# Tables rebuilt on chip for the second pass, diagonal matrices on VectorE, and the mixing inputs loaded by ScalarE's queue

## What is computed

```python
x = x + einsum('bct,bcd->bdt', x, weights[cond])       # mixing: one of 16 matrices per batch
K = 2 * einsum('hn,hnl->hl', Ct, exp(dtA * arange(2048))).real   # 64 complex modes per channel
y = irfft(rfft(x, 4096) * rfft(K, 4096))[..., :2048] + x * D     # causal convolution per channel
x = x + y * (arange(2048) < length[:, None])
```

## Time and profile before

| | us |
|---|---|
| median of 3 runs (lowest, highest) | 1109.16 (1108.6, 1116.84) |
| profiled execution | 1110.37 |
| its span | 1108.4 |
| PE busy in the span | 1021.2 (92%) |
| VectorE busy | 768.2 (69%) |
| ScalarE busy | 573.6 (52%) |
| GpSimd busy | 635.0 (57%) |
| HBM read, written | 171.25 MB, 147.00 MB |

### The profile page before, as it was taken

How to read it: one execution, slowest core, us unless ns; L and a number is a source line. 1 busy time by engine, 2 the same in 40 slices (tenths; PEclk the granted TensorE clock), 3 DMA queues, 4 the chain that set the end, 5 groups by cost and what they waited for, 6 DMA issues and landing times.

```text
span 1108.4 us, 33416 instructions
## 1 busy us (share of the span) xinstructions
PE 1021.2 (92%) x12910; PEld 793.0 (72%) x12910; DVE 768.2 (69%) x1754; ACT 573.6 (52%) x1275; POOL 635.0 (57%) x1377
## 2 busy tenths in 40 slices
PE   8877784889898999899999999999999999999998
PEld 5332242457676667698898988888889888988986
DVE  4989930447565556577777787777777777777775
ACT  2634352335454444456566565555565555555554
POOL 3201136955566465276765868658686676757740
PEclk9999997889999999999999999999999999999999
DMA  9999999899999999989999999999999999899994
GB/s 342 415 408 416 418 414 389 295 361 362 394 372 386 372 388 341 327 211 292 208 261 255 260 264 220 260 226 258 280 229 255 239 254 280 206 263 217 267 215 125
DMA packets 225277, 330.93 MB, mean 299 GB/s; under 512 B 60306, under 2 KB 105746, under 8 KB 216930
## 3 DMA queue, kind: packets, MB, share of 16 engines
q1 hardware_dynamic: 224802, 328.34, 96.9%
q0 software_dynamic: 160, 0.20, 0.1%
q10 hardware_dynamic: 160, 0.26, 0.1%
HBM read 171.25 MB, written 147.00 MB: 287 GB/s over the span
## 4 chain that ended last, share of the span: by engine, by line
PE 74%; DMA 19%; ACT 2%; issue 2%; SPq 2%; DVE 1%; DVEq 0%; ACTq 0%
PE bank L834 15%; PE bank L852 14%; PE bank L796 12%; DMA u_scratch<-stage 10%; PE bank L773 10%; PE bank L813 7%; PE bank L751 7%; DMA u_row<-u_scratch 6%; PE bank L840 5%; PE bank L739 3%; DMA gt_scratch<-gt_sb 2%; ACT stage L935 1%; DMA x_f<-in_x 1%; SPq L400 1%; DVE o_sb L1253 0%
## 5 line engine op out<-in xcount | busy, mean ns | idle before, releaser
L852 PE MATMUL bank<-g_sb,st_sb 128*128 128x256 f16 x1536 | 308.4, 274 | 0.3 <-issue 0.3
L773 PE MATMUL bank<-ident,u_row 128*128 128x128 f32 x1024 | 279.1, 276 | 19.4 <-DMA u_row<-u_scratch 18.3
L636 POOL TENSOR_TENSOR g_sb<-g_x,g_sb 128x128 f16<-128x128 f32 x256 | 115.9, 487 | 265.1 <-ACT g_sb L920 265.1
L964 ACT ACTIVATE st_sb<-bank 128x128 f16<-128x128 f32 x448 | 124.1, 277 | 252.5 <-PE bank L813 182.2
L1253 DVE COPY_PREDICATED o_sb<-mask,u_row 128x512 f32<-128x512 uint8 x256 | 199.1, 778 | 16.2 <-issue 16.0
L1236 DVE TENSOR_TENSOR st_sb<-bank,st_sb 128x128 f16<-128x128 f32 x448 | 130.2, 291 | 113.7 <-ACT st_sb L964 107.7
L1231 DVE SCALAR_TENSOR_TENSOR u_t<-bank,u_t 128x512 f16<-128x512 f32 x256 | 176.0, 688 | 44.4 <-ACT u_t L948 43.5
L834 PE MATMUL bank<-toep,u_t 128*128 128x192 f16 (+1 forms) x1752 | 198.0, 221 | 1.8 <-issue 1.8
L948 ACT ACTIVATE u_t<-bank 128x512 f16<-128x512 f32 x256 | 151.4, 592 | 48.2 <-PE bank L773 48.1
L773 PEld LDWEIGHTS bank<-ident,u_row 128*128 128x128 f32 x1024 | 144.7, 142 | 31.3 <-DMA u_row<-u_scratch 20.8
L739 PE MATMUL bank<-x_f,w_buf 128*128 128x512 f32 x280 | 130.7, 616 | 35.9 <-issue 24.5
(11 more groups left out here) (142 smaller groups left out, 1527.8 us busy)
## 6 DMA issues: line engine op xcount, KB each, us to landing
x_f<-in_x SPq DMA_DIRECT2D x64, 1024.0 KB, 13.4
u_scratch<-stage SPq DMA_DIRECT2D x128, 512.0 KB, 11.3
u_row<-u_scratch SPq DMA_DIRECT2D x128, 512.0 KB, 5.6
out<-o_sb SPq DMA_DIRECT2D x510, 128.0 KB, 3.7
toep<-k_scratch SPq DMA_DIRECT2D x16, 512.0 KB, 7.8
g_scratch<-g_sb SPq DMA_DIRECT2D x12, 512.0 KB, 7.3
gt_scratch<-gt_sb SPq DMA_DIRECT2D x12, 512.0 KB, 7.7
toep_later<-k_scratch SPq DMA_DIRECT2D x24, 256.0 KB, 6.3
```

Of the source, the lines that this page charges most:

```text
L773: ins = pe.transpose(bank[:, u_bank(s, v), k % 4 * P:(k % 4 + 1) * P], ap(u_row[b], v * UNIT + g * Q + tb * P, [[1, P]]), ident[:, :])
L852: last = pe.matmul(bank[:, y, col:col + Q], st_sb[s % 2][:, v, a, gr * P:(gr + 1) * P], g_sb[t % GS][:, h, b, :], start=False, stop=(m == ...
```

## The change

- The second copies of the 12 wide tables are no longer stored and loaded. `store_g`, `load_g`, `load_gt`, `stored_g` and the waits on them go. POOL makes every table when its slot comes, the 24 of the `part` 1 slots too, and `transpose_g` transposes them by DMA.
- A list `MADE_AT` says which tables POOL makes in slot c: those of slot c+2 up to slot 12, later those of slot c+3.
- All diagonal matrices are made by DVE at place 5.2; POOL makes none.
- In slots 0 to 9, ACT issues the loads of `x` right behind its evacuations (`load_x(act, ...)` in `unit_evac`), no longer SP. SP's `load_u(c+1, 1)` moves from behind the four stores at k=0 to before them at k=1.
- Up to slot 10, DVE's overlay of (c-1, 1) moves from place 5.1 to 4.2, and the output work of (c-1, 2) from 7.1 to 6.2 and 6.3.
- The stage buffers of batch 34 are 6 and 7, not 0 and 1.

```diff
+MADE_AT = [[] for _ in range(NSL + 2)]
+for s in range(2, NSL):
+    MADE_AT[s - 2 if s <= LATER + 2 else s - 3] += TABS[s]
...
-STAGE_AT = [m % STAGES if m < 2 * NBW else m % (STAGES // 2) for m in range(2 * NB)]
+STAGE_AT = [m % STAGES for m in range(2 * NBW)] + [0, 1, 2, 3, 6, 7] + [m % (STAGES // 2) for m in range(2 * NBW + 6, 2 * NB)]
...
             if last is not None:
                 eng.wait_ge(s_st, 7 * SLOT_OF[last] + 1)
-                stored_g(eng, last)
...
+        def load_x(eng, n):
+            last = before(X_AT, n)
+            if last is not None:
+                batch_mixed(eng, last)
+            eng.dma_start(x_f[X_AT[n]][:, :], x[n, :, :]).then_inc(s_x[X_AT[n]], 16)
...
             def mixing_slot(c):
                 for k in range(8):
-                    if k == 0:
-                        if c > 0:
-                            load_toeplitz(c)
+                    if k == 0 and c > 0:
+                        load_toeplitz(c)
+                    if k == 1:
+                        load_u(c + 1, 1)
                         if has(c - 2):
                             store_out(sp, c - 2, 1)
-                        load_u(c + 1, 1)
-                    if k == 1:
-                        store_g(c)
...
                     if k == 5:
+                        if c == 0:
+                            stages_landed(sp, (6, 7), NB)
                         load_u(c + 2, 0)
...
-                        if UNITS[u].batch and q == 3 and n + 3 < NB:
-                            load_x(n + 3)
...
-                if c < WIDE:
-                    store_g(c)
                 if c + 1 >= WIDE and has(c + 1):
-                    if SLOTS[c + 1].made:
-                        transpose_g(c + 1)
-                    else:
-                        load_gt(c + 1)
+                    transpose_g(c + 1)
...
                     load_toeplitz(c + 2)
-                    if not SLOTS[c + 2].made:
-                        load_g(c + 2)
...
             def slot(c):
-                if has(c + 2) and SLOTS[c + 2].made:
-                    for t in TABS[c + 2]:
-                        outer(t)
-                if has(c + 1) and not lam_by_dve(c + 1):
-                    for t in TABS[c + 1]:
-                        make_lambda(t)
+                for t in MADE_AT[c]:
+                    outer(t)
...
-                if has(c + 2) and SLOTS[c + 2].made:
-                    for t in TABS[c + 2]:
-                        outer_lo(t)
+                for t in MADE_AT[c]:
+                    outer_lo(t)
...
             def unit_evac(u):
 
                 to, half = unit_copy(act, u)
                 act.activation(to, half, ACT.Copy).then_inc(s_ev, 1)
+                for w in (u - 1, u):
+                    if w >= PROLOGUE and UNITS[w].batch and UNITS[w].part == 3 and UNITS[w].of + 3 < NB:
+                        load_x(act, UNITS[w].of + 3)
...
-                steps = [(0.0, "s", c - 1, 7), (0.1, "u", c, 3), (0.2, "o", c - 2, 3), (0.3, "g", c + 2, 0),
+                steps = [(0.0, "s", c - 1, 7), (0.1, "u", c, 3), (0.2, "o", c - 2, 3), (0.3, "g", c, 0),
...
-                         (4.0, "s", c, 3), (4.1, "u", c + 1, 1), (5.0, "s", c, 4), (5.1, "o", c - 1, 1),
-                         (5.2, "l", c + 1, 0), (6.0, "s", c, 5), (6.1, "u", c + 1, 2), (7.0, "s", c, 6), (7.1, "o", c - 1, 2)]
+                         (4.0, "s", c, 3), (4.1, "u", c + 1, 1), (5.0, "s", c, 4),
+                         (5.1 if c > LATER else 4.2, "o", c - 1, 1), (5.2, "l", c + 1, 0), (6.0, "s", c, 5),
+                         (6.1, "u", c + 1, 2), (7.0, "s", c, 6), (7.1 if c > LATER else 6.3, "o", c - 1, 2)]
...
-                        elif lam_by_dve(of):
+                        else:
                             make_lambda(of)
```

More of the change, by code:

```diff
@@ L2 @@
 from contextlib import ExitStack
-from itertools import accumulate
 from typing import NamedTuple
@@ L57 @@
     part: int
-    made: bool
-SLOTS = [Slot(True, 4 * i, 0, True) for i in range(WIDE)]
+SLOTS = [Slot(True, 4 * i, 0) for i in range(WIDE)]
 for i in range(H // 2 - 2 * WIDE):
-    SLOTS.append(Slot(False, H1 + 2 * i, 0, True))
+    SLOTS.append(Slot(False, H1 + 2 * i, 0))
     if i % 3 == 2 and i // 3 < WIDE:
-        SLOTS.append(Slot(True, 4 * (i // 3), 1, False))
+        SLOTS.append(Slot(True, 4 * (i // 3), 1))
 NSL = len(SLOTS)
@@ L75 @@
         SLOT_OF.append(s)
-MADE_NO = list(accumulate([0] + [int(SLOTS[s].made) for s in SLOT_OF]))
+MADE_AT = [[] for _ in range(NSL + 2)]
+for s in range(2, NSL):
+    MADE_AT[s - 2 if s <= LATER + 2 else s - 3] += TABS[s]
 GT_AT = [t % 2 if t < 2 * WIDE else t % 4 for t in range(len(PAIR_OF))]
@@ L369, in landed_with @@
             return t0 if t > t0 and TOEP_AT[t0] % 4 < 3 and TOEP_AT[t] == TOEP_AT[t0] + 1 else t
-        def loads_of_g(t):
-            return sum(not SLOTS[SLOT_OF[r]].made for r in range(t % GS, t + 1, GS))
         def unit_copy(eng, u):
@@ L406, in _ @@
             sp.dma_start(w_f[:, :, :], w_in.rearrange("s c d -> c s d")).then_inc(s_in[2], 16)
-            def load_x(n):
-                last = before(X_AT, n)
-                if last is not None:
-                    batch_mixed(sp, last)
-                sp.dma_start(x_f[X_AT[n]][:, :], x[n, :, :]).then_inc(s_x[X_AT[n]], 16)
             def store_half(n, j):
@@ L503, in _ @@
             for n in range(1, XS):
-                load_x(n)
+                load_x(sp, n)
             for n in range(FIRST):
@@ L787, in inputs_to_state @@
                         b = GT_AT[t]
-                        landed = sum(32 if SLOTS[SLOT_OF[r]].made else 16 for r in range(2 * WIDE, t + 1) if GT_AT[r] == b)
-                        pe.wait_ge(s_gt[b], landed)
+                        pe.wait_ge(s_gt[b], 32 * (GT_AT[2 * WIDE:t].count(b) + 1))
                 wait(pe, s_stl, 7 * s)
@@ L991, in slot @@
                         unit_evac(of)
+                    elif what == "g":
+                        for t in MADE_AT[of]:
+                            g_hi(t)
                     elif has(of):
@@ L998, in slot @@
                             out_evac(of, k)
-                        elif what == "t":
+                        else:
                             fold_toeplitz(of)
-                        elif SLOTS[of].made:
-                            for t in TABS[of]:
-                                g_hi(t)
             slots(slot)
```

100 lines of the change are left out of this document (25 added, 75 removed).

## The result

The changed kernel takes 1145.78 us in the median of four runs (1143.45 to 1150.53), the kernel before 1113.0 in four (1108.6 to 1120.32). The ratio is 1.029, with a 95% interval of 1.022 to 1.037: slower, as forecast, but by 32.8 us between the medians where the forecast had 15.1, and 0.8 us above the upper end of the range. The profiled execution took 1150.53 us with a span of 1148.4, 40 us more than the span before.

A forecast was written before the change was run, and what follows sets the result against it. PE was taken to bound the long last stretch; the mixing slots held 24 us of waits or low clock. From 1110.37 us, -19 + 21.6 + 12.5 = +15.1 gave 1125.5, median 1124; range 1097 to 1145.

The forecast's parts named there:

- (1): Slots 11 to 62: VectorE's matrices between the states of steps 4 and 5 make PE wait, +21.6 us.
- two matrices take 402.73 - 401.53 = 1.20, one 0.60: Duration of VectorE's diagonal matrix, read in the mixing slots and used past them: 0.60 us each.
- (2): Twelve slots 12 to 56: ScalarE waits 1.96 us for GpSimd's second table, PE about 1.04 us each; +12.5 us.
- the 1.41 us of rows 10: VectorE's idle time before a slot's first state, taken as room that absorbs part of ScalarE's 2.50 us lateness.
- Rival C: Past the mixing: GpSimd slows beside VectorE's new instruction, outer product 6.6 us; +13 us, 1137 us; chance 0.12.
- The mixing slots, -19: Slots with mixing: table-store waits go and waits for rows shrink, -19 us of 24 us idle or low clock.
- the end of -8: Low end of the mixing gain: only slot 10's wait goes, since the DMA engines stay full; -8 us.
- rival B: Mixing slots: the DMA engines stay the bound, -8 us instead of -19, whole 1135 us; chance 0.12.
- I take 1.5 us of these 1.9: Mixing slots: earlier overlay brings the load of rows forward by 1.5 us, leaving 0.4 us of wait per slot.
- their entry at nothing: Mixing slots: ScalarE's 28 issues of x at 0.65 us each counted as costing nothing; uncovered 18 us.
- 13.6: Predicted length of slot 10 without waits, in us.
- no PE wait on them shows: Past the mixing: DMA queues lose 48 loads and gain 48 transposes; 0, at most 2 us either way.

The follow-up runs named there:

- e9: Changed kernel with GpSimd's table instructions past slot 10 cut to two columns, later tables not computed; span 1106.4 us, groups of four slots 48.1 us.
- e2: Kernel before with VectorE making all diagonal matrices, tables still stored and loaded; span 1141.9 us, eleven groups 541.2 us against 517.4.
- e6: Changed kernel with x loads on SyncE, that of step 3 held until the rows are issued at step 5; span 1130.0 us, slots 1 to 11 219.1.
- e1: Changed kernel with the 25 mixing-slot loads of x back on SyncE at their old place; span 1141.9 us, slots 1 to 11 228.7.
- e8: Changed kernel with the mixing slots' whole old order, table stores still gone; span 1140.9 us, slots 1 to 11 224.8.
- e11: Second profile of the kernel of e8; span 1136.6 us, slots 1 to 11 222.8.
- e12: Second profile of the unmodified changed kernel; span 1148.5 us, slots 1 to 11 232.1.
- e3: Changed kernel with three g_x buffers, not two, GpSimd making up to two outer products ahead past slot 10; span 1128.0 us, eleven groups 543.8.

## Why the prediction was right or wrong, point by point

- **Direction: right. Mechanisms: right past the mixing, half right in it.** Both losses past the mixing are there, each at its place: the matrix between two states, and twelve waits of ScalarE on GpSimd of 1.86 us on average (1.96 predicted). In the mixing slots the wait on a table store went, but PE's waits for rows did not.
- **(1), the matrices, +21.6: too small.** The step that failed is "two matrices take 402.73 - 401.53 = 1.20, one 0.60". That row lies where GpSimd stood still (its last instruction there ended at 399.5), and beside a working GpSimd the instruction takes longer: 0.68 and 0.94 us in the 16 and 2 matrices of the mixing slots of the kernel before, so its own trace had the difference. Past the mixing the mean is 0.89 to 0.92 us. The other steps held: without GpSimd beside the matrix a narrow slot lost 0.21 us, in e9 and in e2 (0.31 predicted); with it 0.7. e2 gives the term as 23.8 us in the eleven groups, 27.7 with slots 11 to 15 and 59 to the end (+2.4, +1.5).
- **(2), the second table, +12.5: too small.** The wait itself was sized well, and what PE loses by it was not: 16.4 us in the eleven groups, 1.5 for each and not 1.04. With slot 12, where slots 11 to 15 took 1.7 us more than in e2, it is about 18. The overlay and the matrix on VectorE were longer too, so there may have been less room than the 1.41 us of rows 10; what the missing half microsecond is was not tried.
- **Rival C** named the right cause, GpSimd and VectorE in each other's way, and looked at the wrong engine. Its condition came true: from 520 to 1040 us an outer product took GpSimd 4 x (0.496 + 0.542 + 0.635) = 6.7 us, where C had 6.6, but by the same count it took 6.5 in the kernel before, and ScalarE's waits were no longer than forecast. The dear part was the slower VectorE, in the state chain. The Trainium skill (GPSIMD Engine Reference, Specifications) has the two share SBUF interfaces, with contention when VectorE reads two SBUF inputs; e9's 0.68 us against 0.92 agrees.
- **The mixing slots, -19: too large**, 9.2 measured in the profiled runs, near the end of -8 and so near rival B's time, though not by B's cause: e6 shows that the DMA engines had room for 219 us. The step that failed is "I take 1.5 us of these 1.9" for the earlier overlay, which was to leave 0.4 us of wait in a slot. The load was issued 2 us earlier and landed 0.3 us earlier, because a load of `x` stood right ahead of it (with `x` behind it, in e6, it landed 2.9 us earlier than before the change); PE's waits for rows between 200 and 470 us went from 18.3 to 17.7 us, and the 3.45 us of slot 0 became 4.2. ScalarE's issues of `x` took 0.34 us each, and there were 25, not 28: their entry at nothing is not refuted, since e1, with `x` back on SyncE, has the same landing times. The removed stores alone gave what was forecast for the whole side: in e8 and e11 the span up to slot 11 is 15.4 and 19.2 us shorter than before. The reordering added nothing to that and gave some of it back.
- **Slot 10:** its wait on a store went, and slots 10 to 11 took 17.7 us instead of 21.2, not 13.6: PE waited 2.4 us there for rows, and the clock was at 1.2 GHz for part of it. In e12 the same code took 14.7 us, so the 13.6 is missed by 1 to 4 us.
- **"no PE wait on them shows", DMA transposes at 0:** no such wait shows now either. The further tables cost 2.6 us in the groups (e3 minus e2) and 0.9 behind slot 59, slightly more than "at most 2 us".
- **The sum.** Past the mixing the profile has 49.3 us where the sum had 34.1: 6.1 more by (1), some 5.6 by (2) and 3.5 by the further tables. The mixing side gave 9.8 less. Together these are the 25 us between 1125.5 and 1150.5; between the medians the miss is smaller, 22 us.
- **The range.** I had B and C exclude each other. The result has about the size of both at once: independent misses add.

## What to carry to other kernels

Take the duration of an instruction from a row where the other engines do what they will do beside it: the same instruction on the same tiles took 0.60 us from start to start in one stage and 0.86 in another, and on a chain that closes every 1.17 us, with at most 0.20 us of room, that is more than the margin. Where two runs of one stretch differ, divide it into PE's busy and idle time and read the clock before looking for a cause in the code. Issue what is needed first ahead of what is needed later, whichever queue the latter sits on; a load of 1 MB moved to another queue is not out of the way, and an urgent load issued earlier gains nothing if that puts it right behind one. Before a second producer step is added in front of an in-order consumer, give it one more buffer and let it run ahead: 2 KB a partition were worth 16 us here.

## What the runs showed of the hardware that I had not expected

- VectorE is slower with GpSimd beside it in both of its instructions with two SBUF inputs: the matrix 0.68 and 0.92 us, the overlay 0.74 and 0.82 us (e9 and changed kernel). The copy `x_t`, with one SBUF input, takes 0.70 and 0.74. Its instructions that read PSUM did not change: `u_t` 0.69 and 0.69 us, `st_sb` 0.29 and 0.29.
- The mixing stretch, with the DMA engines near full, varies by several us between profiles of kernels alike in it (223.7 to 233.9), over half of it by the granted clock (0.97 to 1.00); with the loads ordered by need three profiles lie close together and at full clock (218.0, 218.5, 219.1).
- With less to move, the rate in the mixing stretch fell from 362 to 331 GB/s (changed) and 338 (e8). Whether the rows landed sooner by it hung on the order: the load of step 5 took 5.9 us in e8 and e11 where it had taken 7.0, and 8.7 in the changed kernel.
